# A rewritten stage of rows ahead of a RoPE attention: centred operands, a scale inside the rotation, two products instead of four

## The reference, cut to what matters

```python
x = x + _layernorm(_L0_attn_ref(_layernorm(x, axis=-1), ...), axis=-1)
x = x + _layernorm(_L0_ffn_ref(_layernorm(x, axis=-1), ...), axis=-1)
x = x + _layernorm(_L1_attn_ref(_layernorm(x, axis=-1), L1_attn_wq, L1_attn_wk, L1_attn_wv), axis=-1)
x = x + _layernorm(_L1_ffn_ref(_layernorm(x, axis=-1), ...), axis=-1)
```

```python
out = jnp.zeros_like(x).at[jnp.arange(b)[:, None], flat_idx].add(out_tok)
...
out_re = x_re * c - x_im * s
out_im = x_re * s + x_im * c
...
scores = jnp.einsum('bqhd,bkhd->bhqk', q, k) / jnp.sqrt(jnp.asarray(HEAD_DIM, dtype=q.dtype))
```

## Time and profile before

| | |
|---|---|
| median of 3 runs | 6540.49 us (6531.06 to 6551.6) |
| profiled execution, its own time | 6539.95 us |
| its span | 6538.2 us |
| granted clock of TensorE, mean | 0.916 of full speed |
| busy over the span | PE 89%, DVE 77%, ACT 62%, POOL 34% |

### The profile page before, as it was taken

The page is one execution under the profiler, slowest core; times in us unless marked ns, Lnnn a source line. Parts: engine busy times, 40 slices in busy tenths (PEclk is TensorE's granted clock), DMA queues, the critical chain, the costliest instruction groups (busy, mean ns, idle before and its releaser), DMA issues. The chain is left out here.

```text
span 6538.2 us, 115678 instructions
## 1 busy us (share of the span) xinstructions
PE 5811.3 (89%) x39234; PEld 2654.8 (41%) x39234; DVE 5047.6 (77%) x6893; ACT 4055.0 (62%) x7256; POOL 2216.9 (34%) x1098
## 2 busy tenths in 40 slices
PE   5997766675799999999999999988899999999993
PEld 3443551343233333333333333344455555555542
DVE  5997520576899999999899999957677777777745
ACT  3774101111488888888888888865366666666660
POOL 2332100244000000000000000012499999999991
PEclk9998966677799999999999999986799999999995
DMA  4112668254433333333333333239311111111106
GB/s 145 49 49 74 181 208 307 97 170 163 59 51 50 51 51 51 50 51 51 51 51 51 51 50 50 39 90 335 105 41 40 40 40 40 40 40 40 40 6 209
DMA packets 373496, 548.51 MB, mean 84 GB/s; under 512 B 68976, under 2 KB 273456, under 8 KB 353232
## 3 DMA queue, kind: packets, MB, share of 16 engines
q1 hardware_dynamic: 360144, 524.51, 33.1%
q10 hardware_dynamic: 12800, 16.78, 0.7%
HBM read 351.76 MB, written 186.78 MB: 82 GB/s over the span
## 5 line engine op out<-in xcount | busy, mean ns | idle before, releaser
L687 DVE TENSOR_REDUCE at_NM<-at_MX 128x1 f32<-128x1024 f32 (+1 forms) x4096 | 3759.6, 952 | 599.9 <-PE at_MX L520 567.3
L629 ACT ACTIVATE at_PB<-at_S 128x512 f32<-128x512 f32 x6144 | 3283.2, 598 | 901.8 <-PE at_S L549 752.3
L520 PE MATMUL at_MX<-at_KT,at_QT 48*128 48x512 f32 (+1 forms) x6144 | 2383.9, 450 | 92.3 <-DMA at_VS<-v 72.3
L549 PE MATMUL at_S<-at_QT,at_KT 50*128 50x512 f32 (+1 forms) x6144 | 2335.1, 434 | 5.8 <-ACT at_PB L629 5.5
L560 PE MATMUL at_AV<-at_PB,at_VS 128*32 128x256 f32 (+1 forms) x20480 | 1862.0, 435 | 19.0 <-ACT at_AVS L637 13.2
L549 PEld LDWEIGHTS at_S<-at_QT,at_KT 50*128 50x128 f32 (+1 forms) x6144 | 1010.3, 188 | 919.7 <-issue 480.1
L520 PEld LDWEIGHTS at_MX<-at_KT,at_QT 48*128 48x128 f32 (+1 forms) x6144 | 998.4, 190 | 597.2 <-DVE at_NM L687 403.2
L482 POOL TENSOR_TENSOR at_SUM<-at_SUM,at_PB 128x2048 f32<-128x2048 f32 x192 | 883.3, 4601 | 23.7 <-POOL at_SUM L482 0.9
L560 PEld LDWEIGHTS at_AV<-at_PB,at_VS 128*32 128x32 f32 x20480 | 410.2, 108 | 969.7 <-ACT at_PB L629 828.4
L482 POOL TENSOR_TENSOR at_SUM<-at_PB 128x2048 f32<-128x2048 f32 x160 | 752.2, 4703 | 45.7 <-ACT at_PB L629 45.1
L455 POOL CAST at_NMR<-at_NMF 16x128 fp32r<-16x128 f32 x96 | 27.0, 281 | 1638.2 <-ACT at_NMF L642 1638.2
(11 more groups left out here) (173 smaller groups left out, 3892.7 us busy)
## 6 DMA issues: line engine op xcount, KB each, us to landing
moe_W<-in_w SPq DMA_DIRECT2D x64, 1024.0 KB, 10.4
at_QT<-qk SPq DMA_DIRECT2D x384, 128.0 KB, 5.5
at_KT<-qk SPq DMA_DIRECT2D x384, 128.0 KB, 6.9
qk<-r_HI SPq DMA_DIRECT2D x64, 512.0 KB, 5.0
qk<-r_LO SPq DMA_DIRECT2D x64, 512.0 KB, 5.3
at_VS<-v SPq DMA_DIRECT2D x96, 256.0 KB, 8.5
at_QT<-qk SPq DMA_DIRECT2D x96, 256.0 KB, 4.1
at_KT<-qk SPq DMA_DIRECT2D x96, 256.0 KB, 6.2
```

The lines of the kernel that those rows point to most:

```text
L520: ins = nc.tensor.matmul(MX[r][:, a, :], QT[u][h:h + NQ, b * P:(b + 1) * P], KT[u][h:h + NQ, (c + a) * W:(c + a + 1) * W], start=True, sto ...
L549: nc.tensor.matmul(SP_[item(it, s, "score", t)[1]][:, :], KT[u][h:h + NQ + 2, kb * P:(kb + 1) * P], QT[u][h:h + NQ + 2, c * W:(c + 1) * W] ...
L629: nc.scalar.activation(PB[:, t % NPB, :], SP_[r][:, :], ACT.Exp, scale=scale).then_inc(exp_done, 1)
L687: nc.vector.tensor_reduce(NM4[:, b, c:c + 1], MX[r][:, :, :].rearrange("p a n -> p (a n)"), AX_X, ALU.max, negate=True).then_inc(ring_got, 1)
```

## The change

`phase_rope` takes the place of `phase_rows` for this stage, written out for 16 groups without a loop. What it does differently:

- The experts' outputs of all batches are loaded once and centred along the features (`OC`), so rows of `PA` have mean 0 and only their scale is applied, in one fused operation with the addition to `X` (`add`).
- The weights are centred along the input features: a product with a matrix of 1/256 gives their means, and VectorE subtracts them (`WC`). So the rows `X` go to TensorE as they are (`turn`), without mean or scale taken off.
- The second scale (`RS1`) is applied after the projection: inside the two products of the rotation, and in ScalarE's copy of the values.
- The rotation is a product of the pairs in reversed order with a signed sine table into `TS`, a product in place with a cosine table, and one addition into `QR`. Both tables are built on the chip from the plain half of the rope table; the factor 1/4 moves into the exponential of the attention.
- `A` and `X` have three buffers; `PT` is turned and copied in halves; SyncE stores V ahead of queries and keys, two groups later.

```diff
--- before.py
+++ after.py
@@ -1811,6 +1811,364 @@
             values(NGR - 1)
...
+def phase_rope(nc, routed_d, eo_d, x_d, xnew_d, ident_d, w_d, rope_d, qk_d, v_d):
+
...
+            def store_qkv(g):
+                b, e = divmod(g, E4)
+                u = g % 2
+                wait(sp, v_done, 2 * g + 2)
+                out = v_d.rearrange("(b h) p n w -> b p h n w", b=B)[b]
+                sp.dma_start(out[:, :, e * J:(e + 1) * J, :], VB[u][:, :, :, :]).then_inc(l_st[u], 16)
...
+                for a in range(2):
+                    wait(sp, split_done, 4 * g + 2 * a + 2)
+                    for part, tile in enumerate((HI, LO)):
+                        out = qk[a, part].rearrange("(c p) t -> p c t", p=P)
+                        sp.dma_start(out[:, :, e * GT:(e + 1) * GT],
+                                     tile[u][:, 2 * a:2 * a + 2, :].bitcast(F32)).then_inc(l_st[u], 16)
...
+            sp.dma_start(O[:, :, :], eo_d.rearrange("b e d -> e b d")).then_inc(o_ld, 16)
+            load(0)
+            sp.dma_start(WQ[:, :, :], w_d.rearrange("(c p) n -> p c n", p=P)).then_inc(w_ld, 16)
+            sp.dma_start(ident[:, :], ident_d).then_inc(const_ld, 16)
+            sp.dma_start(ROPE[:, :, :, :, :], rope_d).then_inc(const_ld, 16)
+            load(1)
+            for g in range(NGR):
+                if g + 2 < NGR:
+                    load(g + 2)
+                store(g)
+                if g > 1:
+                    store_qkv(g - 2)
...
+            def split(g, k):
+                u = g % 2
+                if k == 0:
+                    wait(pool, l_st[u], 80 * (g // 2))
...
+            for g in range(NGR):
+                if g + 1 < NGR:
+                    scale0(g + 1)
+                if g > 0:
+                    split(g - 1, 0)
+                    split(g - 1, 1)
+                if g + 1 < NGR:
+                    scale1(g + 1)
+                if g > 0:
+                    split(g - 1, 2)
+                    split(g - 1, 3)
...
+            def source(g):
+                u = g % NX
+                wait(pe, a_ld[u], 16 * (g // NX + 1))
+                wait(pe, x_sum, g)
...
+                    ins = nc.tensor.matmul(PA[:, j, :], A[u][:, j * P:(j + 1) * P], OC[:, g // E4, :],
...
+                ins.then_inc(a_done, 1)
+
+            def turn(g):
+                wait(pe, x_sum, g + 1)
+                for c in range(CC):
+                    wait(pe, xt, CC * (g - 1) + c + 1)
+                    for j in range(J):
+                        ins = nc.tensor.transpose(PT[:, c, j * P:(j + 1) * P],
+                                                  X[g % NX][:, j, c * P:(c + 1) * P], ident[:, :])
+                    if c < CC - 1:
+                        ins.then_inc(half_turned, 1)
+                ins.then_inc(turned, 1)
...
+            def turn_qk(g, k):
+                u = g % 2
+                if k == 0:
+                    wait(pe, roped, J * (g + 1))
...
+                nc.tensor.matmul(QK[0][:, :], MEAN[:, :], WQ[:, c, 0:2 * D], start=(c == 0), stop=(c == CC - 1))
+            for c in range(CC):
+                ins = nc.tensor.matmul(PV[:, 0, :], MEAN[:, :], WQ[:, c, 2 * D:3 * D],
+                                       start=(c == 0), stop=(c == CC - 1))
+            ins.then_inc(w_mean, 1)
...
+            for g in range(NGR):
+                turn(g)
+                if g > 0:
+                    turn_qk(g - 1, 0)
+                if g + 1 < NGR:
+                    source(g + 1)
+                if g == 0:
+                    pe.wait_ge(w_cent, 2 * CC)
+                for j in range(J):
+                    project(g, j)
+                    if j % 2:
+                        project_v(g, j // 2)
+                    if g > 0 and j < J - 1:
+                        turn_qk(g - 1, j + 1)
+            for k in range(4):
+                turn_qk(NGR - 1, k)
...
+            def values(g, q):
+                u = g % 2
+                wait(act, vproj, 2 * g + q + 1)
+                wait(act, rs1, g + 1)
+                wait(act, l_st[u], 80 * (g // 2))
+                for jj in range(2):
+                    j = 2 * q + jj
+                    ins = nc.scalar.activation(VB[u][:, :, j, 0:DH], PV[:, jj, :].rearrange("p (h d) -> p h d", d=DH),
+                                               ACT.Identity, scale=RS1[u][:, j:j + 1])
+                ins.then_inc(v_done, 1)
...
+            def add(g):
+                u = g % NX
+                wait(dve, rs0, g + 1)
+                wait(dve, x_ld[u], 16 * (g // NX + 1))
+                for j in range(J):
+                    ins = nc.vector.scalar_tensor_tensor(out=X[u][:, j, :], in0=PA[:, j, :], scalar=RS0[:, j:j + 1],
+                                                         in1=X[u][:, j, :], op0=ALU.mult, op1=ALU.add)
+                ins.then_inc(x_sum, 1)
...
+            def rope(g, j):
+                u, blk, n = g % 2, J * (g % E4) + j, J * g + j
+                heads = [t[:, :].rearrange("p (h i r) -> p h i r", i=DH // 2, r=2) for t in (QK[j % 2], TS[j % 2])]
+                qk, ts = heads
+                cos, sin = (t[:, blk, :, :].unsqueeze(1).to_broadcast([P, 2 * H, DH // 2, 2]) for t in (COS, SIN))
+                wait(dve, proj, n + 1)
+                wait(dve, rs1, g + 1)
+                nc.vector.scalar_tensor_tensor(out=ts, in0=qk[:, :, :, ::-1], scalar=RS1[u][:, j:j + 1], in1=sin,
+                                               op0=ALU.mult, op1=ALU.mult).then_inc(crossed, 1)
+                wait(dve, crossed, n + 1)
+                nc.vector.scalar_tensor_tensor(out=qk, in0=qk, scalar=RS1[u][:, j:j + 1], in1=cos,
+                                               op0=ALU.mult, op1=ALU.mult).then_inc(direct, 1)
+                if j == 0:
+                    wait(dve, qk_put, 4 * (g - 1))
+                wait(dve, direct, n + 1)
+                nc.vector.tensor_tensor(QR[u][:, j, :], QK[j % 2][:, :], TS[j % 2][:, :], ALU.add).then_inc(roped, 1)
...
+            dve.wait_ge(o_ld, 16)
...
+            for b in range(B):
+                ins = nc.vector.tensor_scalar(OC[:, b, :], O[:, b, :], OMV[:, b, 0:1], None, ALU.subtract)
+            ins.then_inc(o_cent, 1)
+            stats_a(0)
+            add(0)
+            stats_x(0)
...
+                nc.vector.tensor_tensor(WC[:, c, 0:2 * D], WQ[:, c, 0:2 * D], QK[0][:, :],
...
+            for r in range(2):
+                nc.vector.tensor_copy(COS[:, :, :, r], ROPE[:, :, 0, 1, :]).then_inc(tables, 1)
+                nc.vector.tensor_scalar(SIN[:, :, :, r], ROPE[:, :, 1, 1, :], 2.0 * r - 1.0, None,
+                                        ALU.mult).then_inc(tables, 1)
+            dve.wait_ge(tables, 4)
+            for g in range(NGR):
+                if g + 1 < NGR:
+                    stats_a(g + 1)
+                rope(g, 0)
+                rope(g, 1)
+                if g + 1 < NGR:
+                    add(g + 1)
+                    stats_x(g + 1)
+                rope(g, 2)
+                rope(g, 3)
+
...
-    phase_rows(nc, "r4", "experts", (routed, expert_out), x1, x2, ident, "rope", (d["wqkv1"], d["rope"], qk1, v1))
-    phase_attention(nc, "at1", HEADS1, DH1, 1.0, qk1, v1, ao1, ident)
+    phase_rope(nc, routed, expert_out, x1, x2, ident, d["wqkv1"], d["rope"], qk1, v1)
+    phase_attention(nc, "at1", HEADS1, DH1, DH1 ** -0.5, qk1, v1, ao1, ident)
```

193 lines of the change are left out of this document (added).

## The result

| | before | after |
|---|---|---|
| median of 4 runs each, same comparison | 6546.05 us | 6438.47 us |
| ratio, 95% interval | | 0.984 [0.981, 0.987] |
| profiled execution: own time, span | 6539.95, 6538.2 us | 6442.2, 6440.4 us |
| first transfer of the first attention | 1624.50 us | 1510.51 us |

The kernel is 107.6 us faster; forecast were 134, at 6406, in a range of 6382 to 6445. The median lies in the range, 32 us above the forecast.

What follows compares the result with a forecast made beforehand. A cycle of waits between VectorE and TensorE was taken as the bound. VectorE's 14.4 us plus 2.7 idle gave 17.1 per group instead of 24.9; with ends, 133.9 us less than 6539.95: forecast 6406, range 6382 to 6445.

Steps and rivals of the forecast that it cites:

- What bounds the kernel, and the size of the stage's part: This stage: a cycle of waits sets the pace, no engine is full; about 440 us of 6538, at most 7%.
- VectorE's prices: VectorE per group: statistics 3.7, rotations 8.8 (2.2 per block), add 1.9, together 14.4 us.
- rival 4: Rotation's in-place and reversed-pair products crawl: slower than before, 0.03; turn-taking alone 6451, in part sharing 0.16 with transfers.
- rival 2: VectorE: dependent operations start as early as independent ones and the add has the fused pitch; 6390, chance 0.14.
- The cycle: Steady round: VectorE's 14.4 us plus 2.7 idle for hops, turn and PA give a period of 17.1 us.
- TensorE's 15.1 fit, with one gap of 2.0: TensorE's work per group, 15.1 us at the high clock, fits the 17.1 us period with one 2.0 us gap.
- rival 1: TensorE's clock stays low at the head of each round: +2.1 us for 14 rounds, 6435; chance 0.22.
- The sum of the profiled execution: Attention starts at 1490.6 instead of 1624.5, 133.9 us less, so 6539.95 becomes 6406.1.
- the first rounds: Stage's start: first statistics at 1193.95, round 0 near 1205.1 with cold projection +1.6, round 1 at 1223.8.
- the end: After round 14's rotations at 1460.5: group 15 done at 1473.4, then a tail of 17.2 to the attention.
- the terms of group 15: Last group at TensorE's pace: 0.5 + 4 x 1.72 + 1.73 + 3 x 0.44 and one rotation of 2.2, about 12.9.
- Rival 3: Transfers return as the bound: late stores add 1 to 2 us per group, 6420 to 6436; 0.16, partly shared.

Runs made afterwards that it cites:

- sbuf_sum_sf: source_first with the rotation's second product written to SBUF instead of back into PSUM, without its wait for the first product: 6385.73 us.
- four_products_sf_fill: source_first with the rotation as four products and two additions again, and TensorE's gap filled with 22 full-row transposes: 6414.11 us.
- fill_part: The changed kernel with TensorE's gap ahead of the first turn of QR filled by three products of 32 rows: 6438.27 us.
- source_first: The changed kernel with the next group's product PA put ahead of the first turn of QR on TensorE: 6390.96 us.
- both: source_first with a semaphore of its own for V's store, and two of the last group's splits made on VectorE: 6373.62 us.
- fill_full: The changed kernel with TensorE's gap ahead of the first turn of QR filled by eight transposes on 128 rows: 6414.56 us.

## Why the prediction came out as it did

**What bounds the kernel, and the size of the stage's part: right.** The gain comes from this stage: 1624.50 - 1510.51 = 114.0 us, forecast 133.9.

**VectorE's prices: right.** 0.74, 0.76 and 0.69 us for the three operations of a rotation (taken 0.74, 0.74, 0.68), 1.65 for the add (1.9, although the sliced stage before has the same fused operation at 1.66, L1740), statistics at 1.42 + 0.38. From TS at 1348.10 to the end of QR at 1350.35 a block takes 2.25 us (2.2). The product in place in PSUM takes 759 ns, against 743 into SBUF in sbuf_sum_sf, and the reversed pairs 742, as in the earlier trace rows: rival 4 did not occur. Of rival 2 the smaller add is true; a dependent operation still starts 0.03 us after its predecessor's end (1348.84 to 1348.87), 0.77 us after its start. In sbuf_sum_sf, without the wait between the two products, the second starts 0.66 us after the first (1399.43 to 1400.09), so here the wait costs 0.1 us.

**The cycle: right at the high clock.** 14.4 + 2.7 = 17.1 was forecast, 16.86 measured (14.2 + 2.67), VectorE's one wait by PA.

**The step that failed** is "TensorE's 15.1 fit, with one gap of 2.0" at a clock near 1. The gap was 1.6 us, and ten of the 14 rounds lost the clock behind it; the prediction put that at nothing, because there is one gap of 2.0 per round. That is rival 1, with 0.22. Its price was too small as well: it put the turn (0.4) and PA (1.76) on VectorE's cycle, 2.1 to 2.2 us per round, and the slow first QK set only into TensorE's sum (19.0). Measured are up to 1.46 for PA, nothing for the turn and 1.87 for the wait for the first QK set. That rival 1 said 6435 against a median of 6438.5 is in part chance: ten rounds were hit instead of 14, eight of them for more (3.24) and two for less (1.65). From the second store of X to the last, 14 x 16.86 = 236.0; the measured 265.3 are 8 x 3.24 + 2 x 1.65 = 29.2 more.

**The sum of the profiled execution.** Forecast 1490.6 for the attention's start, measured 1510.51, + 19.9: the 14 rounds 265.3 instead of 239.4 (+ 25.9), the first rounds - 3.3, the end - 2.7 (33.7 from the last store of X, forecast 36.4, in which the terms of group 15 add up to 12.6 and not 12.9). The other 16.2 us of 6442.2 - 6406.1 lie behind the stage. Of them 12.1 are in the first attention: from its start to the sliced stage's identity load it takes 2739.8 us instead of 2727.7. Its exponentials are unchanged, 598 ns, as forecast; its clock is not the same in every execution. A stretch of 550 us of it, 700 us behind its start, before and after:

```profile
2324.00:2874.00 550.00, 542.72 (x5161) 204.56 (x5157) 518.36 (x452) 475.96 (x890) 18.18 (x40) 0.99 0.35 51
```

```profile
2211.00:2761.00 550.00, 542.16 (x4987) 202.02 (x4985) 501.12 (x436) 459.24 (x858) 17.50 (x39) 0.95 0.33 49
```

In the profiled executions of the twelve kernels here, all with the same work in the attention, this part takes 2718.8 to 2766.0 us (shortest in four_products_sf_fill, longest in fill_part). No tie to the stage's length shows: source_first and sbuf_sum_sf, whose stages are equal within 0.5 us, have 2742.6 and 2726.0. So I do not put it down to the change, and it is why a single execution can't tell 20 us.

**Where the 155 us come from** that lie between before (6546.7) and source_first (6391.0): no single item. By the medians, and in brackets by the stretch from the first store of X to the attention, untouched rows are worth 75 (78), the two-product rotation 58 (75), the fused add 29 (28), each undone alone on source_first, and the order of PA 47 (51). They add up to 209 (231), more than the whole, 156 (164). The likely reason is that each undoing opens a gap on TensorE (0.9 to 2.7 us) and the clock falls behind it in some or all rounds; fillings show this for the rotation and for the order of PA alone.

**Rival 3 (transfers)** did not occur: LO lands in 5.5 us instead of 4.4, and no wait of ScalarE in the steady stretch ends by a transfer. In source_first, at 0.86 of the transfer engines' time, it shows a little: seven such waits, worth the 2.9 us that both takes away.

## What to carry to other kernels

When a wait is forecast on an engine, price it twice: as idle time, and as what TensorE loses behind it, and look which of its next operations the waiting engine needs first. Between two operations of TensorE, put first the one whose inputs are ready and whose output is waited for; here that change of order was worth 47 us. An operation taken off the chain can be worth several times its own duration: the 1.4 to 2.0 us per group of the mean cost 5 us per group.

## What the runs showed that was not expected

- TensorE's clock can fall without idle time. In fill_part it fell in PA, behind 1.56 us of products with 32 rows; in fill_full it stayed, with 1.04 us of transposes on 128 rows and 0.7 us of idle time in the same place.
- Equal rounds need not get equal clock: 1.57 us of idle time stood ahead of PA at 1.99 us and, one round later, of PA at 3.45. The fall comes 0.37 us later in PA from one slow round to the next, until a round escapes it, so how many rounds are hit is not told by the gap alone.
- The shared resource of VectorE and GpSimd is paid by whichever starts second: 1.49 us for an addition of 256 that takes 0.42 alone, or 1.07 for a copy that takes 0.61. So the same inputs cost much or nothing, by 0.1 us of timing.
